# A transformer layer on one core: twelve probability tiles a pair through device memory in place of ten

## The reference

```
attn = softmax(einsum('bhnr,bmhr->bhnm', Q, K))          # per head 256 x 256
x = layernorm(x + einsum('bhnm,bmhd->bnd', attn, V))
h = silu(w1 x * s1) * (w2 x * s2); h = gelu(h1 h * s); h = gelu(h2 h * s)
out = layernorm(x + w3 h * s3)
```

## Time and profile before

| | us |
|---|---|
| median of 3 runs (lowest, highest) | 929.28 (928.76, 932.49) |
| the profiled execution: its own time | 927.26 |
| its span, first to last instruction | 925.1 |
| TensorE busy | 902.8 (98%) |
| ScalarE busy | 867.2 (94%) |
| VectorE busy | 794.9 (86%) |
| GpSimd busy | 685.5 (74%) |

### The profile page before, as it was taken

One profiled execution on the slowest core, in us unless ns is written; L12 is line 12 of the kernel. 1 busy time (PEld: TensorE's weight loads), 2 busy tenths in 40 slices (PEclk: granted clock), 3 DMA queues, 4 the chain that ended last, 5 costly groups with the idle time before them and its releaser, 6 DMA issues.

```text
span 925.1 us, 19419 instructions
## 1 busy us (share of the span) xinstructions
PE 902.8 (98%) x5959; PEld 754.9 (82%) x5959; DVE 794.9 (86%) x1744; ACT 867.2 (94%) x2107; POOL 685.5 (74%) x657
## 2 busy tenths in 40 slices
PE   8989999999999999999999999999999999999995
PEld 6877878878888888888888888888888888788885
DVE  7999688897989889898998989899898988977676
ACT  8968999999999999999999999999999999999763
POOL 6956777778777777878878786877878777785742
PEclk9999999999999999999999999999999999999998
DMA  6006144161532606244260633506154260520110
GB/s 219 1 3 207 45 137 137 61 192 35 174 111 94 183 33 196 67 145 142 68 202 17 195 91 117 170 33 209 45 158 128 87 187 23 188 77 12 35 36 25
DMA packets 133801, 99.18 MB, mean 107 GB/s; under 512 B 13504, under 2 KB 110400, under 8 KB 133696
## 3 DMA queue, kind: packets, MB, share of 16 engines
q1 hardware_dynamic: 133696, 97.91, 34.2%
HBM read 53.03 MB, written 44.83 MB: 106 GB/s over the span
## 4 chain that ended last, share of the span: by engine, by line
PE 79%; DVE 6%; ACT 5%; DMA 4%; issue 3%; SPq 3%; POOL 1%; POOLq 0%; DVEq 0%; ACTq 0%
PE bank L1748 12%; PE bank L1612 12%; PE bank L1749 12%; PE bank L1614 10%; PE bank L1613 10%; PE bank L1672 10%; PE bank L1618 6%; PE bank L1728 2%; PE bank L1729 2%; SPq L380 2%; DMA pt_lo<-crossing 1%; ACT prob L692 1%; DVE neg_max L1117 1%; PE bank L1802 1%; DVE pt_lo L332 1%
## 5 line engine op out<-in xcount | busy, mean ns | idle before, releaser
L460 POOL TENSOR_TENSOR prob<-prob,inv_total 128x512 f32<-128x512 f32 x256 | 270.2, 1068 | 92.8 <-DVE inv_total L1123 91.0
L692 ACT ACTIVATE prob<-bank,neg_max 128x256 f32<-128x256 f32 x512 | 242.2, 516 | 6.3 <-DVE neg_max L1117 4.7
L1117 DVE TENSOR_REDUCE neg_max<-bank 128x2 f32<-128x512 f32 x256 | 169.4, 677 | 0.8 <-PE bank L1672 0.7
L1612 PE MATMUL bank<-pt_hi,v_hi 128*128 128x256 f32 x512 | 149.2, 291 | 0.3 <-DVE pt_lo L332 0.3
L1614 PE MATMUL bank<-pt_hi,v_lo 128*128 128x256 f32 x512 | 144.1, 281 | 0.0
L1613 PE MATMUL bank<-pt_lo,v_hi 128*128 128x256 f32 x512 | 144.0, 281 | 0.0
L692 ACT ACTIVATION_READ_ACCUMULATOR prob<-bank,neg_max 128x1 f32 x512 | 127.2, 248 | 0.0
L332 POOL TENSOR_TENSOR pt_lo<-pt_lo,pt_hi 128x512 fp32r<-128x512 f32 x70 | 91.5, 1307 | 35.6 <-ACT pt_hi L335 35.5
L1612 PEld LDWEIGHTS bank<-pt_hi,v_hi 128*128 128x128 f32 x512 | 96.5, 189 | 11.9 <-issue 2.0
L332 POOL TENSOR_TENSOR even_lo<-gelus,even_hi 128x512 fp32r<-128x512 f32 (+1 forms) x63 | 81.2, 1290 | 33.3 <-ACT even_hi L335 25.0
L332 DVE TENSOR_TENSOR t_lo<-bank,t_hi 128x512 fp32r<-128x512 f32 x128 | 86.7, 679 | 18.0 <-ACT t_hi L335 16.8
(11 more groups left out here) (154 smaller groups left out, 2686.9 us busy)
## 6 DMA issues: line engine op xcount, KB each, us to landing
crossing<-prob SPq DMA_DIRECT2D x140, 256.0 KB, 2.3
pt_lo<-crossing SPq DMA_DIRECT2D x560, 64.0 KB, 2.1
xt_in<-in_x_t SPq DMA_DIRECT2D x16, 256.0 KB, 2.9
res<-in_x SPq DMA_DIRECT2D x16, 256.0 KB, 3.3
passing<-y SPq DMA_DIRECT2D x15, 256.0 KB, 2.1
yt<-passing SPq DMA_DIRECT2D x60, 64.0 KB, 2.0
out_x<-y SPq DMA_DIRECT2D x15, 256.0 KB, 2.7
h_in<-in_h_t SPq DMA_DIRECT2D x2, 1024.0 KB, 8.5
```

Of the source, the lines that this page charges most:

```text
L460: nc.gpsimd.tensor_tensor(tile, tile, by, ALU.mult).then_inc(s_norm, 1)
L692: last = nc.scalar.activation(into, scored, ACT.Exp, bias=neg_max[:, u, nt:nt + 1], accum_out=total[:, u, nt:nt + 1])
L1117: nc.vector.tensor_reduce(neg_max[:, u, :], sc_bank(i, u).rearrange("p (t m) -> p t m", m=N), AX.X, ALU.max, negate=True).then_inc(s_max, 1)
L1612: mm(dst, w_hi, m_hi, start=start, stop=False)
```

## The change

In the middle pairs tiles 14 and 15 also go through device memory. Six tiles have their low part on GpSimd instead of five. `norm2` of whole pairs moves from VectorE to GpSimd; the last pair's halves stay on VectorE and get their own semaphores. All five queues have a new order from first to last, and the bank tables are new. In TensorE's cycle the scores of groups 6 and 7, and of groups 0 and 1 of the next pair, stand directly behind each other. In ScalarE's cycle the four GELUs of layer 3 come in one stretch.

```diff
-SENT = (4, 5, 6, 7, 8, 9, 10, 11, 12, 13)
-POOLED = (4, 6, 8, 10, 12)
+SENT = (4, 5, 6, 7, 8, 9, 10, 11, 12, 13, 14, 15)
+POOLED = (5, 6, 8, 9, 12, 13)
@@ gpsimd (the one on VectorE goes)
+            def norm2(f):
+                if there(f):
+                    hold(pool, s_rs2, f + 1)
+                    for t in range(TT):
+                        last = nc.gpsimd.tensor_scalar(y[:, t, :], y[:, t, :], mv2[:, t, 0:1], rstd2[:, t:t + 1],
+                                                       ALU.subtract, ALU.mult)
+                    last.then_inc(s_y, 1)
...
                 norm(k, 8)
+                norm2(k - 3)
                 norm(k, 9)
@@ sync, the end of the loop
                 prob_out(k, 13)
                 prob_back(k, 12)
                 prob_back(k, 13)
+                prob_out(k, 14)
+                store(k - 3)
+                prob_out(k, 15)
+                prob_back(k, 14)
+                prob_back(k, 15)
                 y_out(k - 2)
                 y_back(k - 2)
@@ scalar, layer 3's GELUs in the loop (exp(k, 6) and what follows come after them)
+                gelu3(k - 2, 0)
+                gelu3(k - 2, 1)
+                high(k - 2, 3, 0)
+                v_high(k, 3)
+                high(k - 2, 3, 1)
                 pt_high(k, 2)
...
                 pt_high(k, 3)
+                gelu3(k - 2, 2)
+                high(k - 2, 3, 2)
+                gelu3(k - 2, 3)
+                high(k - 2, 3, 3)
@@ vector, the last pair
             def stats2_half(b):
                 t = slice(NT * b, NT * (b + 1))
+                dve.wait_ge(s_y, LAST)
```

More of the change, by code:

```diff
@@ L634, in _ @@
             norm(15, 15)
+            low(14, 3, 1)
             rstd2_of(13)
-            low(14, 3, 0)
-            low(14, 3, 1)
+            low(14, 3, 3)
             low(14, 3, 2)
-            low(14, 3, 3)
+            norm2(13)
             rstd1_of(15, 1)
@@ L651, in _ @@
             rstd2_of(14)
+            norm2(14)
             rstd2_half(0)
@@ L817, in _ @@
+            v_high(0, 1)
+            exp(0, 3)
+            t_high(0, 7)
+            v_high(0, 2)
+            exp(0, 4)
+            pt_high(0, 1)
+            v_high(0, 3)
+            v_high(0, 4)
+            weight_high(1)
             exp(0, 5)
[L818 to L819 removed]
+            v_high(0, 5)
             exp(0, 6)
[L821 removed]
+            exp(0, 7)
             pt_high(0, 2)
[L823 removed]
+            pt_high(0, 3)
             t_high(1, 0)
[L825 removed]
+            pt_high(0, 4)
@@ L1216, in y_add @@
                                             ALU.add).then_inc(s_yadd, 1)
-            def norm2(f):
-                if there(f):
-                    hold(dve, s_rs2, f + 1)
-                    norm(y, y, range(TT), mv2, rstd2).then_inc(s_y, 1)
             def x1t_low_half(b):
@@ L1487, in _ @@
-            norm2(12)
-            pt_low(15, 1)
+            pt_low(15, 1)
+            x1t_low(14)
+            inverse(15, 5)
+            t_low(15, 7)
+            silu(14, 0)
+            v_low(15, 1)
+            silu(14, 1)
+            gate(14, 0)
             row_max(15, 6)
-            inverse(15, 5)
             pt_low(15, 2)
+            pt_low(15, 3)
+            gate(14, 1)
             row_max(15, 7)
-            norm1(14, 1)
+            inverse(15, 6)
+            silu(14, 2)
+            gate(14, 2)
@@ new lines, in last @@
+                scores(15, 4, (s_pt_lo, 15, J, 3), (s_gate, 14, KC, 2))
+                turn_prob(15, 4, (s_exp, 15, J, 8))
+                layer1_z2(14, 3, w, (s_gate, 14, KC, 3))
+                values(15, 2, (s_silu, 14, KC, 3))
+                values(15, 3, (s_yt, 13, 1, 1))
+                turn_prob(15, 5, (s_silu, 14, KC, 4))
+                layer2(14, 0, 0, w, (s_gate, 14, KC, 4))
+                turn_prob(15, 6, (s_pt_lo, 15, J, 5))
+                layer2(14, 1, 0, w, (s_exp, 15, J, 9))
@@ L1981, in last @@
+                layer2(14, 0, 1, w)
+                values(15, 4, (s_pt_lo, 15, J, 6))
+                turn_prob(15, 7, (s_v_lo, 15, VT, 3))
+                layer2(14, 2, 0, w, (s_pt_lo, 15, J, 7))
+                layer2(14, 1, 1, w)
+                layer2(14, 3, 0, w, (s_gelu2, 14, KC, 1))
+                layer2(14, 2, 1, w)
+                values(15, 5, (s_v_lo, 15, VT, 4))
                 times_v(15, 4)
-                layer4(13, 1, w)
+                layer2(14, 3, 1, w)
+                scores(15, 5, (s_gelu2, 14, KC, 3), (s_exp, 15, J, 10))
@@ L2141, in _ @@
-            turn_prob(0, 1, (s_exp, 0, J, 5))
-            turn_prob(0, 2, (s_v_lo, 0, VT, 1))
-            query_or_key(1, 0, (s_exp, 0, J, 6))
-            values(0, 3, (s_v_lo, 0, VT, 2))
+            scores(0, 1, (s_t_lo, 0, H, 4))
+            query_or_key(0, 5, (s_t_lo, 0, H, 2))
+            query_or_key(0, 6)
+            values(0, 0, (s_t_lo, 0, H, 5))
+            query_or_key(0, 7, (s_exp, 0, J, 1))
+            turn_prob(0, 0, (s_t_lo, 0, H, 6))
+            values(0, 1, (s_exp, 0, J, 2))
@@ L2145, in _ @@
+            scores(0, 2, (s_exp, 0, J, 3), (s_v_lo, 0, VT, 1))
+            values(0, 2, (s_t_lo, 0, H, 7))
+            values(0, 3, (s_v_lo, 0, VT, 2))
+            turn_prob(0, 1, (s_exp, 0, J, 4))
+            values(0, 4, (s_pt_lo, 0, J, 1))
+            scores(0, 3, (s_exp, 0, J, 5), (s_v_lo, 0, VT, 3))
+            values(0, 5, (s_t_lo, 0, H, 8))
+            scores(0, 4, (s_pt_lo, 0, J, 2), (s_v_lo, 0, VT, 4))
             times_v(0, 0)
-            scores(0, 4, (s_pt_lo, 0, J, 2), (s_exp, 0, J, 7))
```

1230 lines of the change are left out of this document (579 added, 651 removed), and 6 rows, old and new, of the table TURN_OTHER.

## The result

The changed kernel took 967.25 us (median of 4 runs, 959.52 to 969.98) beside 929.51 for the one before (4 runs): ratio 1.0386, 95% interval 1.032 to 1.0453. I had forecast 907, with 900 to 919 as range. It is 3.9% slower.

A forecast was written before the change was run, and what follows sets the result against it. TensorE's own instructions were taken as the bound. 927.3 - 12.3 (fewer transposes) - 11.6 (fewer runs of scores) + 1.4 (returned tiles) = 904.8, and 2.0 to the median: 907 us; the 8-in-10 range was 900 to 919.

The forecast's parts named there:

- TensorE's savings: On TensorE, fewer transposes save 0.88 us a cycle and fewer runs of scores 0.80: cycle from 55.0 to 53.3 us.
- The 26 table loads fewer: On ScalarE, four table loads a pair instead of six: -2.8 us a cycle, leaving 51.8 of 53.3; no gain by itself.
- y's normalisation on GpSimd: Four tensor_scalar moved to GpSimd take 1.2 us a cycle (to 4.3), hidden unless something queued behind is wanted at once.
- Rival C: GpSimd late: normalisation takes 4.3 us, norm(k, 9) comes 3.1 later, 1 a cycle shows: 919 or so; chance 0.08.
- The returned tiles: Tiles back from memory reach ScalarE within half a microsecond of its asking; 0.1 us a cycle, +1.4 in all.
- SyncE's issues: 68 DMAs a cycle at 0.48 us take 33 of 53 us of SyncE's queue, so it has room, but in order.
- rival B's ring: Ring of four returned tiles: tile 15's return waits for tile 11's multiplication, closing a loop; 938 us, chance 0.09.
- rival A: Returned tiles make ScalarE the bound: three waits a cycle are 2.6 us, 1.1 over its room: 920 us; chance 0.12.
- Head and tail: First and last pairs: head 0, +-3 us; tail 0, to +3 if GpSimd needs 4.3 us for the last normalisation.

The follow-up runs named there:

- e17: e7 with only two of the four DMAs of each returned tile issued, so half of its partitions are not refreshed: 907.15 us.
- e7: Changed kernel with y's four tensor_scalar split over three places in GpSimd's list instead of one block, all work done: 927.54 us.
- e2: Changed kernel with y's normalisation of whole pairs nearly left out: one tensor_scalar on two columns instead of four on 128: 921.68 us.
- e5: Changed kernel with two neighbours on VectorE swapped, the low part of tile 4 ahead of the block turn of tile 9: 950.77 us.
- e6: Changed kernel with 20 unused matmuls of 256 columns on TensorE ahead of its wait for tile 4: 958.11 us.
- e15: e7 with ScalarE's high-part copy of returned tiles made from a constant tile, so only the low part waits for the returns: 924.91 us.
- e16: e7 with TensorE's product with the low part of V left out for the twelve returned tiles of the middle pairs: 928.68 us.
- e1: Changed kernel with y's normalisation back on VectorE, behind inverse(k, 11): 962.96 us.
- e3: Changed kernel with y_add(k - 3) six places later on VectorE, behind inverse(k, 5): 970.62 us.

## Why the prediction was wrong

**TensorE's savings: right.** Sums of pitches over five cycles, per cycle, before and in e17: transposes of prob 2.55 and 1.50 us (forecast -0.88), scores 7.06 and 6.67 and all other matmuls 45.43 and 45.15 (forecast together -0.80; a merger saves part on the scores and part on its neighbours' pitches). So 1.05 and 0.67 were saved where I had 0.88 and 0.80; that the sum fits to 0.04 is in part luck. The sums are 55.04 and 53.32: the cycle with nothing late is 53.3, as forecast. The 26 table loads fewer came too; ScalarE is busy 52.3 us of e17's cycle, 0.5 more than the 51.8 I had.

**GpSimd: wrong, the step that failed.** The sum has y's normalisation on GpSimd at nothing, by "It hides unless something queued behind it is wanted at once". It did not hide: in the one block behind norm(k, 8) it cost 40 us beside e7. Its length was wrong too, though e7 shows that the length alone is not what cost: it reads "Nearest is the first, same size: 4 x 0.3 = 1.2 (to 4.3)". Measured 3.15. The affine select of 128x128 was no neighbour of a tensor_scalar that reads two values per partition from memory; VectorE's 498 ns for the same instruction was the better row, and 803 is 1.6 times that. The 498 is itself a mean of unlike ones: 327 ns at least, 336 in the median, 1351 at most, so by the medians it is 2.4 times. The Trainium skill (GPSIMD Engine Reference, 8. Key points) has elementwise work about twice as fast on VectorE; the trace has 1.6 to 2.4, where my 0.3 us against 0.50 would be 0.6.

**Rival C had the right mechanism and the wrong price.** "About 2 of them are slack, so 1 a cycle shows" gave 919. The measured price of the place is 40 us (e7), or 45 against no normalisation at all (e2). I had followed only the tile that waits, tile 9, for whose return I had worked out slack. The engine that waits for it had none: VectorE's next instruction in order, the low part of tile 4, was wanted at once (e5). Two terms came on top that were in no part of the sum, the halved clock behind the hole (9 us, e6) and the subtraction of 2.10 us where it takes 0.65 beside an idle GpSimd. The last agrees with the Trainium skill (GPSIMD Engine Reference, 8. Key points: the two engines share SBUF interfaces when VectorE has two SBUF inputs); it was seen in all 12 cycles, but no run isolates it, and its share of the 40 us is open.

**The returned tiles: wrong by 1.3 us a cycle.** "I put 0.1 us a cycle on it". With the normalisation out of the way 20 us remain (e7 against e17), where I had 1.4. I had counted SyncE's issues (33 of 53 us) as room. A queue that is 60% busy is no room in itself: the trip of the returned tiles (issues, bytes and landings of 2 us, of which e17 leaves out half together) was enough to hold the cycle. It was not rival B's ring: SyncE waited 2.8 us in all for a tile to be multiplied in e7 (16.8 before). Nor was it rival A alone, since e15, in which ScalarE does not wait for returns, won only 3 us. The chain of e16 goes through ScalarE's, GpSimd's and VectorE's orders; which link of the trip is to blame stays open.

**Head and tail.** The last tensor_scalars on y take 3.15 us on GpSimd where VectorE took 1.11; from the last matmul to the end are 10.7 us before and 13.4 in e17, and 11.0 in e1, where VectorE does it. That is the "+3" I had given as a bound, not the 0.

The sum as it should have been: 927.3 - 12.3 - 11.6 + 3 (tail) + 20 (trip) + 40 (place of the normalisation) is 966, and 969.0 was the run that was profiled. The 20 and the 40 are differences between runs, so only the rest is a test: 927.3 - 12.3 - 11.6 + 3 is 906.4, with the 2.0 to the median 908.4, and e17 took 907.15.

## What to carry to other kernels

When work is put into a queue, price what stands behind it on each engine that will wait, one engine further than the first: the harm came not to the tile that was held but to the unrelated instruction behind it on a third engine. Look for gaps in the queue by the profile and split the work over them; here the same four instructions cost 45 us in one block and 6 in three pieces, tail included. Look also at what will run beside them: beside two-input work on GpSimd VectorE's subtractions took up to three times as long (2.10 us against 0.65), in e5 six times. And once several engines are each within a few per cent of the cycle, a wait in the trace is no measure of what its removal gives: relieve a whole resource to find the holder before reordering anything.

## What was not expected of the hardware

A tensor_scalar with two per-partition operands on 128x128 float32 took GpSimd 0.80 us and VectorE 0.50 on average (0.34 in the median); the same form on two columns still took GpSimd 0.39 (e2), so by an estimate from these two sizes about half of it does not depend on the columns. TensorE's granted clock fell to 0.50 for some 3 us after holes of 2.6 us (after 11 of 12 in the changed kernel, 4 of 11 in e3), and stayed at 1.00 when discarded matmuls filled them. A subtraction of 128x512 from SBUF on VectorE took 0.65 us on average with GpSimd idle beside it and up to 2.10 in the changed kernel and 3.82 in e5; the longest of these ended 0.55 us after the last of two or three two-input instructions that stood back to back on GpSimd, as if it had to let all of them go first.
